# Output product of a linear attention on two row halves and two PSUM banks, with steps of TensorE and VectorE in another order

## What is computed

```python
qkv = _conv(x, w_qkv)
agg = _conv(_conv(qkv, w_dw, groups=C3), w_pw, groups=3 * DIM)
qkv = jnp.concatenate([qkv, agg], axis=1)
...
q = jax.nn.relu(q)
k = jax.nn.relu(k)
v = jnp.concatenate([v, jnp.ones_like(v[:, :, :1])], axis=2)
vk = jnp.einsum('bhds,bhes->bhde', v, k)
out = jnp.einsum('bhde,bhes->bhds', vk, q)
out = out[:, :, :-1] / (out[:, :, -1:] + EPS)
out = out.reshape(B, -1, H, W)
y = _conv(out, w_proj)
```

## Time and profile before

| | us |
|---|---|
| time, median of 3 runs | 2083.55 |
| lowest and highest | 2082.44, 2092.64 |
| span of the profiled execution | 2098.0 |

### The profile page before, as it was taken

How to read it: one execution, slowest core, us unless ns; L and a number is a source line. 1 busy time by engine, 2 the same in 40 slices (tenths; PEclk the granted TensorE clock), 3 DMA queues, 4 the chain that set the end, 5 groups by cost and what they waited for, 6 DMA issues and landing times. The chain is left out here.

```text
span 2098.0 us, 41985 instructions
## 1 busy us (share of the span) xinstructions
PE 1827.5 (87%) x16164; PEld 1232.6 (59%) x16164; DVE 1367.7 (65%) x2786; ACT 892.1 (43%) x2341; POOL 166.5 (8%) x61
## 2 busy tenths in 40 slices
PE   2699999999999999996988989999982589999998
PEld 1355555556666666664766766666651366666676
DVE  3677777766555556441334437777875899999983
ACT  0344444454444444452444445455541134444433
POOL 1000000000000000000000000000001333333321
PEclk9899999999999999997999999999995699999998
DMA  3112222255667657578999986545513001111101
GB/s 100 39 63 78 96 97 78 78 149 159 199 176 202 182 158 205 146 190 199 230 223 254 250 226 168 133 125 139 155 47 127 16 32 63 62 62 62 47 32 46
DMA packets 262635, 267.16 MB, mean 127 GB/s; under 512 B 208868, under 2 KB 234852, under 8 KB 262440
## 3 DMA queue, kind: packets, MB, share of 16 engines
q1 hardware_dynamic: 252040, 225.68, 38.9%
q10 hardware_dynamic: 10240, 38.54, 5.9%
q0 software_dynamic: 160, 0.26, 0.0%
HBM read 148.84 MB, written 115.61 MB: 126 GB/s over the span
## 5 line engine op out<-in xcount | busy, mean ns | idle before, releaser
L499 DVE TENSOR_TENSOR vk<-p_vk,mask_vo 128x512 f32<-128x512 f32 x256 | 176.4, 689 | 476.1 <-PE p_vk L390 476.1
L426 PE MATMUL p_dw<-tw,qd 98*64 98x98 f32 x3072 | 242.9, 294 | 61.2 <-ACT agg_out L694 29.1
L426 PEld LDWEIGHTS p_dw<-tw,qd 98*64 98x64 f32 x3072 | 199.0, 205 | 125.3 <-ACT agg_out L694 46.1
L667 ACT ACTIVATE half_b<-p_qkv 98x384 f32<-98x384 f32 x256 | 125.5, 490 | 236.5 <-PE p_qkv L349 225.8
L694 ACT ACTIVATE agg_out<-p_dw 128x294 f32<-128x294 f32 x256 | 106.8, 417 | 280.1 <-PE p_dw L426 264.4
L452 PE MATMUL p_g<-o,w_proj 128*128 128x392 f32 x512 | 208.7, 533 | 3.0 <-DVE var L555 2.4
L349 PE MATMUL p_qkv<-w_qkv,half_a 128*98 128x384 f32 x512 | 191.4, 497 | 6.7 <-DVE half_a L571 6.7
L349 PE MATMUL p_qkv<-w_qkv,z_odd 128*98 128x384 f32 x512 | 190.5, 495 | 1.8 <-DVE z_odd L571 1.8
L1486 POOL TENSOR_TENSOR gapped<-z,gate_gap 128x1568 f32<-128x1568 f32 x16 | 53.8, 3364 | 1578.0 <-DMA z<-z_scratch 1576.2
L402 PE MATMUL p_out<-vk,qr 128*49 128x136 f32 x2048 | 170.2, 287 | 8.3 <-DVE oN L514 5.6
L711 ACT ACTIVATE o<-p_turn 128x196 f32<-128x196 f32 x256 | 85.5, 334 | 174.5 <-PE p_turn L411 173.8
(11 more groups left out here) (191 smaller groups left out, 3130.7 us busy)
## 6 DMA issues: line engine op xcount, KB each, us to landing
qkv_scratch<-half_b SPq DMA_DIRECT2D x32, 1176.0 KB
qd<-qkv_scratch SPq DMA_DIRECT2D x64, 588.0 KB
agg_scratch<-agg_out ACTq DMA_DIRECT2D x128, 294.0 KB, 5.5
tw<-in_w_toep SPq DMA_DIRECT2D x128, 220.5 KB
half_a<-agg_scratch SPq DMA_DIRECT2D x48, 392.0 KB, 7.1
half_b<-agg_scratch SPq DMA_DIRECT2D x48, 392.0 KB, 6.9
half_a<-in_x SPq DMA_DIRECT2D x16, 784.0 KB, 4.7
x_scratch<-xb SPq DMA_DIRECT2D x16, 784.0 KB, 5.3
```

The costliest lines, as they stand in the source:

```text
L426: mm = pe.matmul(p_dw[NP * cp:NP * cp + NP, PR * s:PR * s + PR], qd[:, QB % 2, :, ch - QB_CH * qb], tw[:, SB % 2, :, 6 * (F % SB_FILLS) + ...
L499: v.tensor_tensor(dst[:, :, 0:128].rearrange("p k (c n) -> p k c n", c=HC), src[:, :, 0:2 * D].unsqueeze(2).to_broadcast([128, 4, HC, 2 * D]),
L667: a.activation(raw[:, e, w, :], p_qkv[r][0:PR, 0:QKV], ACT.Copy).then_inc(raw_ev, 1)
```

## The change

The masked state vk now has 64 + 4 columns instead of 128 + 8: a row half (64 channels, four heads) holds only its own four heads. The output product of an image becomes two products, one for each row half of 64 rows, of 68 columns, and the two halves write different banks; p_out is now two banks. The state product has no bank of its own any more: it is written into the first bank of p_out, into columns that the output product leaves free, and waits for on_ok of the group before (`wait(pe, on_ok, G)`). den, rden and oN are indexed by half and image pair, with as many elements as before, and mask_vo and the constants follow.

On PE, the output product of g-3 and the first fill move to the head of the step, ahead of the first p_qkv; the state product of g-2 moves ahead of the second p_qkv. On DVE, the norm of g-3 moves from behind slot b to behind v_k, ahead of slot a. ACT and SP are not changed.

```diff
--- before.py
+++ after.py
@@ -24,7 +24,7 @@
 PR = 2 * S
 HC = 4
 VC = 2 * D + 1
-VO = 128 + 8
+VO = 64 + 4
 QKV = 3 * 128
 NP = 64
 QB_FILLS, SB_FILLS, DB_FILLS = 16, 4, 4
@@ -222,9 +222,9 @@
         kT = sb("kT", [PR, 2, 2, 128])
         vT = sb("vT", [PR, 2, 2, 2, HC, VC])
         vk = sb("vk", [128, 2, 2, 2, VO])
-        rden = sb("rden", [128, 2, 8])
-        den = sb("den", [128, 2, 8])
-        oN = sb("oN", [128, 2, 2, 128])
+        rden = sb("rden", [128, 4, 4])
+        den = sb("den", [128, 4, 4])
+        oN = sb("oN", [128, 2, 2, 2, 64])
         stat = sb("stat", [128, 2, KT * NB])
         mean = sb("mean", [128, KT, NB])
         var = sb("var", [128, KT * NB])
@@ -234,9 +234,11 @@
         error = sb("error", [128, KT * NB])
 
         p_qkv = [ps("p_qkv0"), ps("p_qkv1")]
-        p_turn, p_vk, p_out, p_dw = ps("p_turn"), ps("p_vk"), ps("p_out"), ps("p_dw")
+        p_turn, p_dw = ps("p_turn"), ps("p_dw")
+        p_out = ctx.enter_context(nc.psum_tensor("p_out", [128, 2, 512], f32))
         p_g = [ps("p_g0"), ps("p_g1")]
-        out_of = p_out[:, :].rearrange("p (r n) -> p r n", r=2)
+        out_of = p_out[:, :, :].rearrange("p r (q n) -> p (r q) n", q=2)
+        vk_of = p_out[:, 0, :].rearrange("p (k n) -> p k n", k=4)[:, :, VO:VO + VC]
         turned_of = p_turn[:, :].rearrange("p (r n) -> p r n", r=2)
 
         def tiles(ap):
@@ -385,9 +387,10 @@
                 pe.wait_ge(k_ok, G + 1)
             pe.wait_ge(v_ok, 2 * (G + 1))
             wait(pe, vk_ev, 2 * G)
+            wait(pe, on_ok, G)
             for pr in range(2):
                 for c in range(HC):
-                    mm = pe.matmul(p_vk[32 * c:32 * c + 32, 2 * VC * pr:2 * VC * pr + 2 * VC],
+                    mm = pe.matmul(vk_of[32 * c:32 * c + 32, 2 * pr:2 * pr + 2, :],
                                    kT[:, G % 2, pr, 32 * c:32 * c + 32], vT[:, G % 2, pr, :, c, :],
                                    start=True, stop=True)
             mm.then_inc(vk_mm, 1)
@@ -399,8 +402,9 @@
             for pr in range(2):
                 for i in range(2):
                     at = PR * pr + S * i
-                    mm = pe.matmul(out_of[64 * i:64 * i + S, pr, 0:VO], qr[:, G % 4, at:at + S], vk[:, G % 2, pr, i, :],
-                                   start=True, stop=True)
+                    for r in range(2):
+                        mm = pe.matmul(out_of[64 * i:64 * i + S, 2 * r + pr, 0:VO], qr[64 * r:64 * r + 64, G % 4, at:at + S],
+                                       vk[64 * r:64 * r + 64, G % 2, pr, i, :], start=True, stop=True)
             mm.then_inc(out_mm, 1)
 
         def pe_out_turn(pe, G):
@@ -408,7 +412,7 @@
             wait(pe, o_ev, G)
             pe.wait_ge(qr_ok, min(G + 4, GT))
             for pr in range(2):
-                mm = pe.transpose(turned_of[:, pr, 0:128], oN[:, G % 2, pr, :], W["ident"][:, :])
+                mm = pe.transpose(turned_of[:, pr, 0:128], oN[:, G % 2, pr, :, :].rearrange("p r n -> p (r n)"), W["ident"][:, :])
             mm.then_inc(ot_mm, 1)
 
         def pe_fill(pe, F):
@@ -463,20 +467,20 @@
                 if F is not None:
                     pe_fill(pe, F)
 
+            if 0 <= g - 3 < GT:
+                pe_out(pe, g - 3)
+            fill(0)
             if 0 <= g < GA:
                 pe_qkv(pe, g, 0)
             if 0 <= g - 1 < GA:
                 pe_q_turn(pe, g - 1)
             elif GA <= g - 1 < GT:
                 pe_pointwise(pe, g - 1)
+            if 0 <= g - 2 < GT:
+                pe_vk(pe, g - 2)
             if 0 <= g < GA:
                 pe_qkv(pe, g, 1)
             pe_slot(pe, g, "a")
-            if 0 <= g - 2 < GT:
-                pe_vk(pe, g - 2)
-            fill(0)
-            if 0 <= g - 3 < GT:
-                pe_out(pe, g - 3)
             pe_slot(pe, g, "b")
             fill(1)
             if 0 <= g - 4 < GT:
@@ -495,25 +499,24 @@
             v.wait_ge(vk_mm, G + 1)
             wait(v, out_mm, G - 1)
             dst = vk[:, G % 2, :, :, :].rearrange("p r i n -> p (r i) n")
-            src = p_vk[:, 0:4 * VC].rearrange("p (k n) -> p k n", k=4)
-            v.tensor_tensor(dst[:, :, 0:128].rearrange("p k (c n) -> p k c n", c=HC),
-                            src[:, :, 0:2 * D].unsqueeze(2).to_broadcast([128, 4, HC, 2 * D]),
-                            W["mask_vo"][:, 0:128].rearrange("p (c n) -> p c n", c=HC).unsqueeze(1).to_broadcast([128, 4, HC, 2 * D]),
+            v.tensor_tensor(dst[:, :, 0:64].rearrange("p k (c n) -> p k c n", c=2),
+                            vk_of[:, :, 0:2 * D].unsqueeze(2).to_broadcast([128, 4, 2, 2 * D]),
+                            W["mask_vo"][:, 0:64].rearrange("p (c n) -> p c n", c=2).unsqueeze(1).to_broadcast([128, 4, 2, 2 * D]),
                             ALU.mult).then_inc(vk_ev, 1)
-            v.tensor_tensor(dst[:, :, 128:VO], src[:, :, 2 * D:VC].to_broadcast([128, 4, 8]),
-                            W["mask_vo"][:, 128:VO].unsqueeze(1).to_broadcast([128, 4, 8]),
+            v.tensor_tensor(dst[:, :, 64:VO], vk_of[:, :, 2 * D:VC].to_broadcast([128, 4, 4]),
+                            W["mask_vo"][:, 64:VO].unsqueeze(1).to_broadcast([128, 4, 4]),
                             ALU.mult).then_inc(vk_ev, 1)
 
         def v_norm_out(v, G):
             v.wait_ge(out_mm, G + 1)
-            v.tensor_scalar(den[:, :, :], out_of[:, :, 128:VO], 1e-15, None, ALU.add).then_inc(den_ok, 1)
+            v.tensor_scalar(den[:, :, :], out_of[:, :, 64:VO], 1e-15, None, ALU.add).then_inc(den_ok, 1)
             v.wait_ge(den_ok, G + 1)
             v.reciprocal(rden[:, :, :], den[:, :, :]).then_inc(rden_ok, 1)
             v.wait_ge(rden_ok, G + 1)
             wait(v, ot_mm, G - 1)
-            v.tensor_tensor(oN[:, G % 2, :, :].rearrange("p r (h d) -> p r h d", h=8),
-                            out_of[:, :, 0:128].rearrange("p r (h d) -> p r h d", h=8),
-                            rden[:, :, :].unsqueeze(3).to_broadcast([128, 2, 8, D]), ALU.mult).then_inc(on_ok, 1)
+            v.tensor_tensor(oN[:, G % 2, :, :, :].rearrange("p q r (h d) -> p q r h d", h=4).rearrange("p q r h d -> p r q h d"),
+                            out_of[:, :, 0:64].rearrange("p k (h d) -> p k h d", h=4),
+                            rden[:, :, :].unsqueeze(3).to_broadcast([128, 4, 4, D]), ALU.mult).then_inc(on_ok, 1)
 
         def group(key):
 
@@ -647,12 +650,12 @@
         def v_step(v, g):
             if 0 <= g - 1 < GA:
                 v_k(v, g - 1)
+            if 0 <= g - 3 < GT:
+                v_norm_out(v, g - 3)
             v_slot(v, g, "a")
             if 0 <= g - 2 < GT:
                 v_vk(v, g - 2)
             v_slot(v, g, "b")
-            if 0 <= g - 3 < GT:
-                v_norm_out(v, g - 3)
             v_slot(v, g, "c")
 
 
@@ -910,7 +913,7 @@
                 for pr in range(2):
                     v.tensor_copy(vT[:, n, pr, :, :, 2 * D:VC].rearrange("p i c o -> p i (c o)"),
                                   W["image_of"][:, :].unsqueeze(2).to_broadcast([PR, 2, HC])).then_inc(ones_ok, 1)
-            v.memset(p_out[:, :], 1.0).then_inc(ones_ok, 1)
+            v.memset(p_out[:, :, :], 1.0).then_inc(ones_ok, 1)
             v.wait_ge(ones_ok, 5)
             for g in range(FIRST, LAST + 1):
                 v_step(v, g)
@@ -1624,7 +1627,7 @@
     g = np.arange(32)
     return {
         "c_mask8": (p[:, None] // GS == p[None] // GS).astype(f),
-        "c_mask_vo": np.concatenate([p[:, None] // D == p[None] // D, p[:, None] // D == np.arange(8)[None]], 1).astype(f),
+        "c_mask_vo": np.concatenate([p[:, None] // D % 4 == p[None, 0:64] // D, p[:, None] // D % 4 == np.arange(4)[None]], 1).astype(f),
         "c_ident": np.eye(128, dtype=f),
         "c_image_of": (pair_image[:, None] == np.arange(2)[None]).astype(f),
         "c_earlier": (np.arange(C)[None, None] < (128 * np.arange(KT)[None, :, None] + p[:, None, None])).astype(f),
```

## The result

| | before | after |
|---|---|---|
| time, median of 4 runs each | 2084.49 | 2252.78 |
| lowest and highest | 2082.44, 2092.64 | 2250.24, 2255.91 |
| span of the profiled execution | 2098.0 | 2249.8 |
| mean granted clock | 0.949 | 0.93 |

The ratio is 1.0795, with a 95% interval of 1.0757 to 1.0833: the kernel is 8% slower, 168 us. The forecast was 2210, with its own range of 2185 to 2235, and the range that should hold 8 in 10 was 2130 to 2280. The result lies in the wide range and above the narrow one; rival (4), 2244, came nearest.

What follows compares the result with a forecast made beforehand. The prediction took PE, which runs in order, as the bound. Its terms 29 + 54 + 12 + 32 = 127 us on the 2098.0 span gave 2225, less 14.5 for the median 2210; range 2185 to 2235, 8 in 10 within 2130 to 2280.

Steps and rivals of the forecast that it cites:

- rival (4): Idle PE takes the clock down more, B at 0.91 rather than 0.98: 34 us more, 2244; chance 0.12.
- D: Steps 177 to 255, without fills: later norm and p_out outside ACT's shadow, 32 us longer, bounds 8 and 40.
- A: Steps 0 to 67, without fills: p_vk waits for the norm, 29 us with steps after B, bounds 5 and 40.
- B: Steps 68 to 122, 128 fills: second fill waits for ACT to empty p_dw, 54 us longer, bounds 27 and 65.
- C: Steps 134 to 176, other fills but three: a third of 35 us taken, 12 us longer, bounds 0 and 35.
- turnings: PE changing between product shapes: 0.16 to 0.18 us more per step, and 0.32 more in B and C.
- the wait for on_ok: The state product waits for the norm of the same step's output product: 3 us within the term of B.
- plain ones: Steps of 2.80 us in D: p_out leaves ACT's shadow, so a plain step can't be under 3.2 us.
- (1): New waits are hidden and only PE's own account remains: 0.08 x 256 = 20 us off, 2063; chance 0.07.
- (2): The output product's row halves don't overlap: 0.22 x 256 = 57 us more, 2267; chance 0.12.
- (3): Engines catch up so later waits are shorter, and transfers bound C: about half the sum, 2150; chance 0.18.
- 14.5 us: How far the median 2083.55 lay below the profiled span 2098.0; carried over, it turned 2225 into 2210.

Runs made afterwards that it cites:

- e4: The changed kernel, but ACT empties the first fill at the head of its step, ahead of the raw copy: 2158.4 us, ratio 1.0333 to the kernel before.
- e11: The kernel before, its orders kept, with the row-half layout only where no fill is near and the state product there in p_dw: 2058.3 us, ratio 0.9864.
- e2: The changed kernel with PE's first fill moved back behind slot a: 2189.4 us, ratio 1.0499 to the kernel before.
- e7: The changed kernel with p_out behind the q turn, and the state product and first fill back behind slot a: 2269.1 us, ratio 1.0853.
- e8: The kernel before with the first fill at the head of the step on PE, and ACT emptying it at the head of its own: 2115.7 us, ratio 1.0128.
- e6: The changed kernel with both row halves' operands read from the first half, so all output products use one row group: 2308.0 us, ratio 1.1057.
- e9: The kernel before with only VectorE's new order, the norm ahead of slot a: 2274.2 us, ratio 1.0876.
- e10: The kernel before with only PE's new order, VectorE and layout as before: 2321.5 us, ratio 1.1108.
- e12: As e7, with slot a ahead of the norm again on VectorE: 2304.5 us, ratio 1.1059 to the kernel before.
- e5: The changed kernel with all output products of one row half ahead of the other's in the program: 2261.1 us, ratio 1.0801 to the kernel before.

## Where the prediction was right and where not

**Right.** Slower, and by the mechanism of the sum. D: 32 forecast, 32.5 measured. The 32 are 10.5 rounds, which is 84 steps, and D has 79; by its own 3.0 us a round D comes to 30. By step of a round (208 to 215) 4.44, 3.67, 3.36, 3.47, 4.76, 3.50, 5.18 and 3.87 were measured, against 4.6, 3.75, 3.24, 3.7, 4.55, 3.4, 5.1 and 3.8. A with the steps behind B: 29 forecast, 27.6 measured. C: 12 and 10.3; that agreement is luck, since a third was a choice, and e4 shows that C can be 10 us below before when ACT empties the first fill early (and e11 that it moves by 6 us with nothing changed in it).

**Mis-sized: B, 54 forecast, 82 measured.** The waits were sized well, partly by errors that cancel. PE's waits for agg_out grew by 51 us (12.4 to 63.6); the sum had 8.8 - 2.5 + 0.8 = 7.1 a round of idle PE, 49 in 6.9 rounds. But the waits that the prediction lists by place add up to 9.3 a round and not to 8.8, and the 2.5 of today are those of the weight loads; PE's own are 12.4 / 6.9 = 1.8. And 7.1 with the 0.10 a step that it gave to turnings is 7.9 a round, not the 7.4 that went into the sum, so that B's term should have been 57 by its own parts. The step that failed is that the term of B left the clock at 0.98, where it came to 0.93. I had that apart, as rival (4), with 34 us for 0.91. From e4, the clock's part is 23.1 us. The turnings and the wait for on_ok, 5 us of the forecast, lie within the 8.6 that e4 still has. In the round of steps 80 to 87 the waits in places 0, 4 and 5 are 1.54, 1.54 and 3.08 us, against 1.56, 1.56 and 3.1 forecast, and yet step 84 is 3.1 us longer than before: 1.54 of wait and 1.5 of half-clock blocks. Rival (4) should not have been a rival: it follows from the forecast's own idle time, and the two add. 54 + 23 = 77 of the 82.

**Under-sized: steps 129 to 133, 8.3 us.** The prediction has no term for them, unless they are the five steps that D's 10.5 rounds have too many, 2 us. Steps 129 to 131 are plain ones, 3.36 us instead of 2.80 each, 1.7 us in all. Then the second set of fills begins and waits for a load, 4.12 us where it was 1.7 before:

```profile
1060.32 1.25 PE L430 MATMUL p_dw<-tw,qd 98*64 98x98 f32 x12 [4.12 <-DMA qd<-qkv_scratch]
```

A fill at the head of the step asks for its data earlier in the step. With the fill back behind slot a (e2, e7) the stretch is 23.9 and 24.0, and with ACT's edit alone (e4) it is 27.8. e8, the old order with the fill at the head, has 24.0, 3.6 more than before, which would fit; but e11, with no fill moved, has 23.9. So the stretch moves by some 3.5 us for reasons that no run here isolates, and the share of the fill's place stays open.

**Turnings, priced well.** They are read from the starts of records: the time from the end of one block's streaming (its last start plus 2 x columns / 2.4 GHz) to the next block's first record, and what that block's first records take longer than the others. After, this is 0.14 us from the output turn into the new p_out (0.096 + 0.042), about 0.2 from p_out to a fill, 0.20 from p_vk to p_qkv and 0.21 from p_dw to p_qkv, within 0.03 of what was taken. Here the rule that was weighed in the prediction held (the Trainium skill, "TensorEngine Tiling (Array Packing)", Key Properties: changing the tiling mode drains the array). p_out and a fill both have 64-column groups. With full rows, before, p_out followed a fill in 0.04 us; with 64-row groups it is 0.17 (medians of 99 and 58 places).

**The rivals.** (1), hidden waits: out, with 51.7 and 93.4 us of them on PE; its 0.08 us a step does not follow from the prediction's own turnings either (0.05 saved in A and D, 0.10 lost in B and C is about nothing in all), and e11's gain of 28 us comes with the old order, where no turning is added. (2), no overlap: out, by e6. (3), elastic waits: out in A, B and D, where waits were as long as carried. (4) held in kind, on top of the forecast, with 23 us where it had 34 and a clock of 0.93 where it had 0.91.

**From span to median.** I took 14.5 us off, as if the profiled execution's excess stayed. The profiled execution of after lies 3.0 below its median, 1.8 of it because a time is that much longer than its span. 8.6 of the 14.5 stood in the untouched last stretch; that its clock was 0.98 could have told. It hid part of the gap: stage by stage the sum is 127 against 160.9 us.

**Of my expectations,** those of e7, e8, e9, e10 and e12 were off: I reasoned on one engine's order with the other's taken as elastic. e9 and e10 were the plainest: I held that DVE's order hardly mattered in the old kernel.

## What to carry to other kernels

Before a bank is shared to make room for a faster product, follow who must be done before it can be written again: here the state product came to wait for VectorE's norm, and that cost 30 us net in stage A alone, as much as the narrower product saves in all in the best version (28 us). When a step is moved on one in-order engine, ask which evacuation releases its buffer, and move that one too: one instruction moved on ScalarE took 94 us off the 168. And where a forecast puts idle time on TensorE at many places of a stage, add the half clock to that same forecast rather than to a rival.

## What the runs showed of the hardware

- Row groups run together though all products of one half stand ahead of the other's in the program (e5: records in fours, 0.47 us for the block, against 0.72 and records in twos on one row group, e6).
- 68-column products on two row and two column groups ran four at a time: 16 records in 0.46 us, a wave each 0.058 us.
- Changing from full-row to 64-row products cost 0.17 us behind a fill, where two full-row products had 0.04 between them.
- With waits of 1.5 to 3 us in about half of the steps of stage B, the granted clock fell from 0.98 to 0.93, and the lost clock was worth 23 us against 50 of idle time. A wait of 1.54 us was once followed by half-clock blocks and once, in the same round, not.
